# Last image: four score banks and two row buffers for the sampling chain, image 6's outputs behind the convolution

## Time and profile before

| what | value |
|---|---|
| time, median of 3 runs | 3008.57 us (3002.29 to 3011.41) |
| profiled execution, own time | 3005.0 us |
| its span, first to last instruction | 3003.2 us |
| PE busy | 2771.4 us, 92% |
| DVE busy | 2201.0 us, 73% |
| ACT busy | 1665.8 us, 55% |
| POOL busy | 197.3 us, 7% |
| chain that ended last | PE 73%, DVE 12%, ACT 5%, DMA 4%, issue 4% |
| mean granted TensorE clock | 0.971 |

### The profile page before, as it was taken

How to read it: one execution, slowest core, us unless ns; L and a number is a source line. 1 busy time by engine, 2 the same in 40 slices (tenths; PEclk the granted TensorE clock), 3 DMA queues, 4 the chain that set the end, 5 groups by cost and what they waited for, 6 DMA issues and landing times.

```text
span 3003.2 us, 60746 instructions
## 1 busy us (share of the span) xinstructions
PE 2771.4 (92%) x25208; PEld 1948.6 (65%) x25208; DVE 2201.0 (73%) x2934; ACT 1665.8 (55%) x2429; POOL 197.3 (7%) x157
## 2 busy tenths in 40 slices
PE   6999799999999999999999999999999999998858
PEld 5666576756667577665776667765677756765434
DVE  5676577687875877868877778768787588775856
ACT  2653466375653755636665556636566375554625
POOL 0000001000200002000020000200020000200300
PEclk9999899999999999999999999999999999998968
DMA  5233012421233112340224311232123311105040
GB/s 202 66 74 107 36 43 76 135 81 45 59 95 130 48 54 60 89 174 8 65 59 134 113 43 39 80 130 86 45 52 101 131 48 54 38 12 175 13 110 29
DMA packets 149602, 235.85 MB, mean 79 GB/s; under 512 B 78609, under 2 KB 97556, under 8 KB 145460
## 3 DMA queue, kind: packets, MB, share of 16 engines
q1 hardware_dynamic: 148468, 219.39, 23.7%
q10 hardware_dynamic: 864, 12.58, 1.2%
HBM read 177.08 MB, written 54.84 MB: 77 GB/s over the span
## 4 chain that ended last, share of the span: by engine, by line
PE 73%; DVE 12%; ACT 5%; DMA 4%; issue 4%; another core or an unknown queue 1%; SPq 0%; DVEq 0%; POOL 0%; ACTq 0%
PE banks L708 12%; PE banks L648 10%; PE banks L677 9%; PE banks L695 8%; PE banks L638 6%; PE banks L894 5%; PE banks L750 5%; PE banks L904 4%; PE banks L896 4%; PE banks L895 4%; DMA recips_dram<-recips 3%; DVE neg_max L1432 3%; DVE exps_turned L1443 2%; ACT exps L1111 2%; PE banks L867 2%
## 5 line engine op out<-in xcount | busy, mean ns | idle before, releaser
L1432 DVE TENSOR_REDUCE neg_max<-banks 128x1 f32<-128x1024 f32 x512 | 601.8, 1217 | 88.8 <-PE banks L677 86.0
L1111 ACT ACTIVATE exps<-banks,neg_max 128x1024 f32<-128x1024 f32 x512 | 566.8, 1113 | 47.4 <-DVE neg_max L1432 46.3
L1123 ACT ACTIVATE exps_turned<-banks 128x1024 f32<-128x1024 f32 x256 | 262.3, 1025 | 553.2 <-PE banks L695 544.9
L1443 DVE COPY exps_turned<-banks 128x1024 f32<-128x1024 f32 x256 | 313.2, 1223 | 262.3 <-PE banks L695 247.5
L677 PE MATMUL banks<-qk_halves 64*128 64x512 f32 x3072 | 432.9, 412 | 60.7 <-ACT exps L1111 39.6
L708 PE MATMUL banks<-exps_turned,values 128*64 128x256 f32 x4096 | 481.1, 384 | 0.8 <-issue 0.8
L695 PEld LDWEIGHTS banks<-ident,exps 64*128 64x128 f32 x8192 | 311.5, 139 | 199.1 <-issue 171.3
L695 PE MATMUL banks<-ident,exps 64*128 64x64 f32 x8192 | 366.6, 228 | 31.4 <-DVE exps_turned L1443 27.3
L708 PEld LDWEIGHTS banks<-exps_turned,values 128*64 128x64 f32 x4096 | 280.3, 137 | 138.8 <-issue 5.1
L677 PEld LDWEIGHTS banks<-qk_halves 64*128 64x128 f32 x3072 | 292.4, 189 | 109.9 <-issue 75.8
L1613 DVE SCALAR_TENSOR_TENSOR qk_halves<-banks,qk_halves 128x1024 fp32r<-128x1024 f32 x256 | 302.0, 1219 | 67.2 <-ACT qk_halves L1160 66.9
(11 more groups left out here) (187 smaller groups left out, 3388.9 us busy)
## 6 DMA issues: line engine op xcount, KB each, us to landing
wqk_ring<-wqk_split SPq DMA_DIRECT2D x62, 512.0 KB
wo_halves<-wo_split_dram SPq DMA_DIRECT2D x8, 2048.0 KB, 7.8
exps_turned<-in_x SPq DMA_DIRECT2D x32, 512.0 KB, 5.6
x_dram<-exps SPq DMA_DIRECT2D x32, 512.0 KB, 2.6
exps_turned<-x_dram SPq DMA_DIRECT2D x32, 512.0 KB, 6.0
out<-exps_turned SPq DMA_DIRECT2D x32, 512.0 KB, 2.6
recips_b<-recips_dram SPq DMA_DIRECT2D x240, 64.0 KB, 3.4
x_image<-in_x SPq DMA_DIRECT2D x14, 1024.0 KB, 7.0
```

The source lines that it names most:

```text
L1111: freed(act.activation(PB[:, 2 * h + n % 2], slot(("s", m, i)), ACT.Exp, bias=NM[:, m:m + 1], accum_out=SS[:, m:m + 1]), ("s", m, i))
L1432: dve.tensor_reduce(NM[:, m:m + 1], slot(("s", m, i)), AX.X, ALU.max, negate=True).then_inc(mx, 1)
L1443: dve.tensor_copy(PT[:, n // 2 % 2, 1, :, P * j:P * j + P].rearrange("p k (r q) -> p k r q", r=2), TB.rearrange("p r (k q) -> p k r q", k= ...
```

## The change: what it does

Only the work of the last image, and the outputs of image 6 beside it, change; for all other images the new helpers return what stood there. All four parts of the convolution follow each other on DVE. The results of image 6 come later: two behind `weights_turned`, two behind `key_blocks`. The second strip on PE follows both `similarities`. The steps of the sampling chain write four banks of the ring in turn, and the rows of half 1 are kept in a second buffer (where `x_hi` lay), so both halves of a step are issued together. SP stores image 6 behind `load_rows`, and waits for all its stores before it loads the residual. `point_outputs`, which writes banks 4 and 5, waits for all results of image 6.

```diff
+        ROWS_MORE = at("rows_more", [P, C], AT_XH)
...
+        def mid_bank(use, j):
+            return PS[:, use % 4] if j == B - 1 else MB
+
+        def rows_kept(f, j):
+            return ROWS_MORE if j == B - 1 and f else PW
...
-                if i:
+                if 0 < i < B - 1:
                     store(i - 1)
             load_out_weights(B)
             rows_to_dram(B - 1)
             for part in range(2):
                 load_rows(part, B - 1)
+            store(B - 2)
+            sp.wait_ge(y_out, 64 * (B - 1))
             load_residual(B - 1)
             move_point_outputs(B)
...
             def offsets(j):
                 pe.wait_ge(gelu_done, j + 1)
                 if j + 1 < B:
                     pe.wait_ge(piece_free, (j + 1) * MAXES + 3)
+                else:
+                    wait_emptied(pe, ("lq", CT - 2, j))
+                    wait_emptied(pe, ("lq", CT - 1, j))
...
             def sample(f, j):
...
-                wait_after(pe, kv_done, 2 * j + f)
+                wait_after(pe, kv_done, 2 * j + (f if j + 1 < B else 0))
                 for r in range(4):
                     for t in range(CT):
-                        mm = pe.matmul(MB[32 * t:32 * t + 32, P * r:P * r + P], WT[:, 4 * f + r, t],
+                        mm = pe.matmul(mid_bank(2 + f, j)[32 * t:32 * t + 32, P * r:P * r + P], WT[:, 4 * f + r, t],
...
-            def turn_rows():
+            def turn_rows(use, f, j):
                 for r in range(4):
-                    mm = pe.transpose(MB[:, P * r:P * r + P], PW[:, P * r:P * r + P], IDENT[:])
+                    mm = pe.transpose(mid_bank(use, j)[:, P * r:P * r + P], rows_kept(f, j)[:, P * r:P * r + P], IDENT[:])
                 return mm
...
             def similarities(f, j):
                 pe.wait_ge(kz_done, j + 1)
-                wait_after(pe, sim_done, 2 * j + f)
+                wait_after(pe, sim_done, 2 * j + (f if j + 1 < B else 0))
...
-                if i:
+                if 0 < i < B - 1:
                     window_outputs(1, i - 1)
             offsets(B - 1)
             turn_weights(B - 1)
             for f in range(2):
                 sample(f, B - 1)
+            for f in range(2):
                 turn_sampled(f, B - 1)
             sampled_keys(B - 1)
             for f in range(2):
                 similarities(f, B - 1)
+            window_outputs(1, B - 2)
+            for f in range(2):
                 turn_similarities(f, B - 1)
+            pe.wait_ge(y_done, CT * (B - 1))
             for f in range(2):
                 point_outputs(f, B)
...
             def keep_sampled(f, j):
                 act.wait_ge(kvt_full, 2 * j + f + 1)
-                act.activation(PW[:], MB, ACT.Copy).then_inc(kvt_done, 1)
+                act.activation(rows_kept(f, j)[:], mid_bank(2 + f, j), ACT.Copy).then_inc(kvt_done, 1)
...
-                for t in range(2 if i else 0):
+                for t in range(2 if 0 < i < B - 1 else 0):
                     result(t, i - 1)
...
-                for t in range(2, CT if i else 0):
+                for t in range(2, CT if 0 < i < B - 1 else 0):
                     result(t, i - 1)
...
             weights_turned(B - 1)
+            for t in range(2):
+                result(t, B - 2)
             sampled(0, B - 1)
             sampled(1, B - 1)
             key_blocks(B - 1)
+            for t in range(2, CT):
+                result(t, B - 2)
             sim_rows(0, B - 1)
             sim_rows(1, B - 1)
             point_blocks(B - 1)
```

More of the change, by code:

```diff
@@ L759, in offsets @@
                     pe.wait_ge(piece_free, (j + 1) * MAXES + 3)
+                else:
+                    wait_emptied(pe, ("lq", CT - 2, j))
+                    wait_emptied(pe, ("lq", CT - 1, j))
                 for t in range(CT):
-                    mm = pe.matmul(MB[0:64, 4 * t:4 * t + 4], TG[:, t], PWZ[:], start=(t == 0), stop=True,
+                    mm = pe.matmul(mid_bank(0, j)[0:64, 4 * t:4 * t + 4], TG[:, t], PWZ[:], start=(t == 0), stop=True,
                                    skip_group_check=True)
@@ L771, in turn_weights @@
                 for t in range(CT):
-                    mm = pe.transpose(MB[:, P * t:P * t + P], PW[:, P * t:P * t + P], IDENT[:])
+                    mm = pe.transpose(mid_bank(1, j)[:, P * t:P * t + P], PW[:, P * t:P * t + P], IDENT[:])
                 mm.then_inc(pw_turned, 1)
@@ L792, in turn_sampled @@
                 pe.wait_ge(kvt_done, 2 * j + f + 1)
-                turn_rows().then_inc(kv_full, 1)
+                turn_rows(f, f, j).then_inc(kv_full, 1)
             def sampled_keys(j):
@@ L797, in sampled_keys @@
                 for t in range(CT):
-                    mm = pe.matmul(MB[:, 64 * t:64 * t + 64], WKB[:, t], KV[:, t],
+                    mm = pe.matmul(mid_bank(2, j)[:, 64 * t:64 * t + 64], WKB[:, t], KV[:, t],
                                    start=(t == 0), stop=True, skip_group_check=True)
@@ L807, in similarities @@
                         c0 = (t * WIN + 2 * (4 * f + r)) * 8
-                        mm = pe.matmul(MB[32 * t:32 * t + 32, P * r:P * r + P], KZR[:, c0:c0 + 32],
+                        mm = pe.matmul(mid_bank(3 + f, j)[32 * t:32 * t + 32, P * r:P * r + P], KZR[:, c0:c0 + 32],
                                        A[:, t, P * (4 * f + r):P * (4 * f + r) + P], start=(r == 0), stop=True,
@@ L814, in turn_similarities @@
                 pe.wait_ge(simt_done, 2 * j + f + 1)
-                turn_rows().then_inc(sim_full, 1)
+                turn_rows(1 + f, f, j).then_inc(sim_full, 1)
             def point_outputs(f, k):
@@ L1132, in tanh @@
                 act.wait_ge(off_full, j + 1)
-                act.activation(OFF[:], MB[0:64, 0:16], ACT.Tanh).then_inc(off_done, 1)
+                act.activation(OFF[:], mid_bank(0, j)[0:64, 0:16], ACT.Tanh).then_inc(off_done, 1)
             def keep_sampled(f, j):
                 act.wait_ge(kvt_full, 2 * j + f + 1)
-                act.activation(PW[:], MB, ACT.Copy).then_inc(kvt_done, 1)
+                act.activation(rows_kept(f, j)[:], mid_bank(2 + f, j), ACT.Copy).then_inc(kvt_done, 1)
             def keep_similarities(f, j):
                 act.wait_ge(simt_full, 2 * j + f + 1)
-                act.activation(PW[:], MB, ACT.Copy).then_inc(simt_done, 1)
+                act.activation(rows_kept(f, j)[:], mid_bank(3 + f, j), ACT.Copy).then_inc(simt_done, 1)
             def log(j):
@@ L1569, in weights_turned @@
                 for g in range(2):
-                    src = MB[64 * g:64 * g + 64].rearrange("p (t z b u e) -> p z b t u e", t=CT, z=2, b=PXT, u=2)[:, 0]
+                    src = mid_bank(1, j)[64 * g:64 * g + 64].rearrange("p (t z b u e) -> p z b t u e", t=CT, z=2, b=PXT, u=2)[:, 0]
                     for w in range(2):
@@ L1589, in key_blocks @@
                     ins = dve.tensor_scalar(KZ[rows, :, :, 4 * g:4 * g + 4],
-                                            MB[rows, 0:256].rearrange("p (t u e) -> p t u e", t=CT, u=WIN),
+                                            mid_bank(2, j)[rows, 0:256].rearrange("p (t u e) -> p t u e", t=CT, u=WIN),
                                             D ** -0.5, None, ALU.mult)
@@ L1606, in sim_rows @@
                     ins = dve.tensor_copy(SM[rows, 16 * f:16 * f + 16],
-                                          MB[rows].rearrange("p (n z u e) -> p n z u e", z=2, u=2, e=8)[:, :, 0, w])
+                                          mid_bank(1 + f, j)[rows].rearrange("p (n z u e) -> p n z u e", z=2, u=2, e=8)[:, :, 0, w])
                 ins.then_inc(sim_done, 1)
```

2 lines of the change are left out of this document (1 added, 1 removed).

## The result

The changed kernel takes 2989.03 us against 3003.81 us before (medians of 13 runs each), a ratio of 0.9945 (95% interval 0.9927 to 0.9963): 14.8 us less where 7.8 were forecast, below the range. In a second comparison of the same two kernels the ratio was 0.9968 (0.9949 to 0.9987).

A forecast was written before the change was run, and what follows sets the result against it. PE bounds the whole span (92% busy), but the last image's stretch is bound by a chain of hand-overs. Convolution 7.8 us earlier, chain length unchanged: 7.8 us off a mean of 3006.8 gives 2999, range 2996 to 3002.

The forecast's parts named there:

- Convolution: Last image's convolution on DVE: done 7.84 us earlier, with both moved products at 2.25 us beside POOL.
- From gelu to the turned weights, early results, waits on PE: Behind the convolution: same length, 7.8 us earlier; early results hidden on DVE, PE's new waits cost nothing.
- Sampling chain: From turned weights to `point_outputs`: length unchanged at 21.9 us, since strip and results put back what overlapping the halves saves.
- Rival 1: Clock rises in the denser chain: up to 6.2 us on strip, first `point_outputs` and bias network's start, to 2993; chance 0.18.
- Outputs: `point_outputs` and bias network's start: clock might lose 1.45 us at one and win 3.0 at the other; neither taken.
- rival 2: Clock falls worse: second `point_outputs` at half clock, 1.45 us more, bias network 1.6 more, to 3002; chance 0.15.
- Transfers: On SP's queue: residual issued by 2891.3, point outputs landed by 2912.6 at worst, needed at 2913.2; free, 0.6 us to spare.
- The sum's base: The total: 7.8 us less, forecast from 3006.8 us, the mean of four times of the kernel before, giving 2999.

The follow-up runs named there:

- two_gaps: The changed kernel with two more waits on PE, before the second sample batch and the second batch of similarities; tail 158.02 us against 150.03 for the changed kernel.
- conv_first: The reordering alone against the kernel before, with the sampling chain's halves still taking turns in one bank and one row buffer; ratio 0.9991, tail 160.80 us.
- best_no_sp: The changed kernel with useless products filling PE's waits and the second strip before the similarities, SP's order unchanged; tail 145.16 us against 150.03 for the changed kernel.

## Why the prediction was wrong

- *Convolution: right.* 7.84 us forecast, 8.08 measured. The moved products met POOL at 2.13, not 2.25; without POOL they take 1.82. By the rule of the Trainium skill (SBUF — State Buffer, section "Who interferes with whom") POOL should have been held up in turn, and the trace agrees in kind: with two more products beside them its eight sums went from 11.40 to 14.55 us.

```profile
2847.67 14.55 POOL L632 TENSOR_TENSOR pixels<-pixels,ln_b 128x512 f32<-128x512 f32 x8
```

- *From gelu to the turned weights, early results, waits on PE: right.* 9.77 against 9.65; `sampled` was released by the turns.
- *Sampling chain: here it failed,* 21.9 us forecast and 16.23 measured. "I take 3.7, as the clock is at half in all of the chain before, and the strip itself didn't raise it" carried the clock of a chain full of gaps over to one without, for the strip and, unsaid, for turns, keys and similarities. Piece by piece against the forecast: both samples 3.7 (3.9), turns 1.35 (2.24), keys 1.15 (2.0), similarities 1.95 (3.91), strip 2.0 (3.74). That is 5.7 us on PE alone; what DVE does in the chain came out as forecast, and `two_gaps` shows the forecast's length when the clock stays down.
- *Rival 1* named this mechanism at 0.18, with its sum in the wrong places: strip 1.7 (right), first `point_outputs` 1.45 (0.7), the bias network's start 3.0 (0.2, and at full clock 1.1 to 1.4), and nothing for turns, keys and similarities, where 3.7 us lay. The evidence set against it, that 3.69 us of the strip hadn't raised the clock, held for the strip (it didn't in `conv_first` and `two_gaps` either) and was carried over to the sample batches, a product of another form.
- *Outputs: not taken, and 1.1 lost.* The second `point_outputs` ran at half clock (3.78), as rival 2 had it.
- *Transfers: right for the wrong reason.* The stores, issued behind the row loads, took 9.4 us and not 2.8, so the residual went out at 2899.80 where 2891.3 had been the latest, and the point outputs at 2901.60, not when ACT had kept them. SP's next work found them landed at 2911.17; ACT's fifth unit came at 2912.12. The residual took 5.7 us and not 17.2 at worst. A microsecond was left of the cover, and `best_no_sp` used it up. The rows are SP's and ACT's timelines, then the transfers with the median us to landing:

```profile
2899.80 1.76 SPq L505 DMA_DIRECT2D exps_turned<-x_dram  x4
2901.60 0.72 SPq L521 DMA_DIRECT2D point_outputs_dram<-point_outputs  x1
...
2912.12 0.69 ACT L1195 ACTIVATE mlp_hidden_more<-banks,mlp_b 128x512 f32<-128x512 f32 x1
...
out<-exps_turned SPq DMA_DIRECT2D x4, 512.0 KB, 9.4
exps_turned<-x_dram SPq DMA_DIRECT2D x4, 512.0 KB, 5.7
...
point_outputs_dram<-point_outputs SPq DMA_DIRECT2D x1, 1024.0 KB, 9.6
```

- *The sum's base.* The mean of four times, 3006.8, stands against a median of 3003.8 over 13 runs. Of the 10 us by which the forecast lies high that is 3.0, the tail's gain beyond the forecast 4.9, and 2.1 is what the medians differ by more than the two profiles (14.8 against 12.65), within their scatter.

## What to carry to other kernels

Where work is packed so that TensorE no longer pauses, don't carry over the clock that its pieces had: work out the sum at both levels and let the range hold both. In this case no rule foretold the level, since the clock rose behind some stretches without a gap and not behind others. A wait of under a microsecond between two batches can cost several times its length. Where a total scatters more than the change is worth, compare the length of the stage that was changed, from profiles.

## What was not expected of the hardware

- With two waits of 0.81 us TensorE stayed at 0.50 for the whole chain, where the same order without them was granted 1.00: 8 us of tail.
- Work without a gap was not enough for that: six microseconds of similarities, strip and turns in `two_gaps`, and four in `conv_first`, ran at 0.50 to their end.
- The same program's tail agreed to 0.02 us in one pair of executions (150.03, 150.05) and differed by 3.3 in another (162.68, 165.94), by where the clock rose and fell; with the order of the transfers changed and nothing else, by 3.9 (153.92).
- The start of the tail, with the same work in front of it, lay between 2834.3 and 2856.0 us over the 14 profiles. That is as wide as the spread of the 13 times of the kernel before (22.0 us). What makes it stays open, but the mean granted clock of the execution goes with it: of the changed kernel's 13 runs the four at 0.971 and 0.972 took 2992.9 to 2996.1 us, the five at 0.975 and 0.976 2978.3 to 2985.3.
